# Expert stage of a graph layer: one half of the gated rows turned by VectorE in squares of 32 by 32

## What is computed

```python
xn = _layernorm(x, axis=-1)
x = x + _L0_gnn_ref(xn, src, dst, ...) + _L0_mix_ref(xn[None], ...)[0]
x = x + _L0_ffn_ref(_layernorm(x, axis=-1)[None], L0_ffn_router_w, L0_ffn_w_gate, L0_ffn_w_up, L0_ffn_w_down)[0]
```

```python
logits = flat @ router_w.T
topk_vals, topk_idx = jax.lax.top_k(logits, K)          # K = 2 of E = 8
topk_w = jax.nn.softmax(topk_vals, axis=-1)
dense_w = jnp.zeros((s, E)).at[jnp.arange(s)[:, None], topk_idx].add(topk_w)
g = jnp.einsum('sd,edh->esh', flat, w_gate)             # 512 -> 1024
u = jnp.einsum('sd,edh->esh', flat, w_up)
y = jnp.einsum('esh,ehd->esd', jax.nn.silu(g) * u, w_down)   # 1024 -> 512
out = jnp.einsum('esd,se->sd', y, dense_w)
```

## Time and profile before

| | |
|---|---|
| time before, median of 3 runs | 1580.67 us |
| the profiled execution's own time | 1579.48 us |
| its span, first to last instruction | 1577.8 us |
| TensorE busy | 1401.8 us (89%), 463.05 of the 474 us from 1103 to 1577 |
| VectorE busy | 915.8 us (58%), 147.19 of those 474 us |
| ScalarE busy | 638.9 us (40%), 59.89 of those 474 us |
| GpSimd busy | 757.0 us (48%), 95.69 of those 474 us |
| transposes of the gated rows, L1713 | 168, 26.3 us busy |

### The profile page before, as it was taken

The page is one execution under the profiler, slowest core; times in us unless marked ns, Lnnn a source line. Parts: engine busy times, 40 slices in busy tenths (PEclk is TensorE's granted clock), DMA queues, the critical chain, the costliest instruction groups (busy, mean ns, idle before and its releaser), DMA issues.

```text
span 1577.8 us, 24763 instructions
## 1 busy us (share of the span) xinstructions
PE 1401.8 (89%) x6831; PEld 659.2 (42%) x6832; DVE 915.8 (58%) x2194; ACT 638.9 (40%) x1124; POOL 757.0 (48%) x776
## 2 busy tenths in 40 slices
PE   6566998867769999999999999782999999999997
PEld 4243444334324444444444444462433334433333
DVE  8745665568737777777777777665332233322332
ACT  2354555545426665666656666540111111111111
POOL 3777777777766655666556665102511111111111
PEclk8677999979879999999999999895999999999999
DMA  4875333333268888888888888852123542514512
GB/s 149 321 256 162 112 113 116 115 113 111 102 219 256 248 247 247 251 250 247 247 249 250 250 247 222 262 217 70 21 81 126 186 156 57 180 41 166 187 25 85
DMA packets 130351, 274.52 MB, mean 174 GB/s; under 512 B 21129, under 2 KB 67933, under 8 KB 129346
## 3 DMA queue, kind: packets, MB, share of 16 engines
q0 software_dynamic: 49872, 150.16, 31.8%
q1 hardware_dynamic: 80434, 123.84, 23.5%
HBM read 211.55 MB, written 64.99 MB: 175 GB/s over the span
## 4 chain that ended last, share of the span: by engine, by line
PE 64%; POOL 21%; issue 7%; DVE 3%; DMA 3%; ACT 0%; SPq 0%; DVEq 0%; POOLq 0%; ACTq 0%
POOL edge_list L423 20%; PE psum L1190 19%; PE psum L1706 17%; PE psum L1718 9%; PE psum L1203 7%; PE psum L1198 5%; PE psum L1185 2%; PE psum L1713 1%; POOL slot_list L1638 1%; DMA shared<-node_table,shared 1%; PE psum L1368 1%; DMA z_rows<-z 1%; PE psum L1369 1%; DVE zN L1785 1%; PE psum L1293 1%
## 5 line engine op out<-in xcount | busy, mean ns | idle before, releaser
L1094 POOL DMA_INDIRECT shared<-node_table,shared x343 | 324.3, 945 | 222.3 <-DVE msg L1162 131.2
L423 POOL DMA_INDIRECT edge_list<-rec,place x313 | 316.8, 1012 | 99.6 <-issue 95.1
L1164 DVE TENSOR_TENSOR msg<-shared,psum 128x768 f32<-128x768 f32 x339 | 321.0, 947 | 0.0
L1190 PE MATMUL psum<-wf,hT 128*128 128x512 f32 x678 | 316.0, 609 | 2.0 <-ACT psum L1124 2.0
L1706 PE MATMUL psum<-shared,zT 128*64 128x512 f32 (+1 forms) x960 | 299.7, 598 | 9.6 <-DVE zT L1779 9.4
L1124 ACT COPY psum<-bias 128x512 f32<-128x512 f32 x343 | 202.1, 590 | 227.8 <-DVE msg L1164 209.1
L1162 DVE TENSOR_TENSOR msg<-shared,psum 128x256 f32<-128x256 f32 x339 | 140.7, 415 | 145.5 <-PE psum L1190 142.0
L1190 PEld LDWEIGHTS psum<-wf,hT 128*128 128x128 f32 x678 | 122.8, 191 | 160.0 <-issue 139.7
L1706 PEld LDWEIGHTS psum<-shared,zT 128*64 128x64 f32 (+1 forms) x960 | 112.6, 159 | 179.0 <-issue 169.4
L440 PE MATMUL psum<-wf,fT 128*128 128x512 f32 (+1 forms) x158 | 100.8, 725 | 80.6 <-DVE rec L767 77.2
L1718 PE MATMUL psum<-shared,hidT 128*64 128x512 f32 (+1 forms) x480 | 152.7, 597 | 0.0
(11 more groups left out here) (304 smaller groups left out, 1531.6 us busy)
## 6 DMA issues: line engine op xcount, KB each, us to landing
shared<-edge_list SPq DMA_DIRECT2D x356, 130.0 KB
shared<-in_L_ffn_w_gate SPq DMA_DIRECT2D x8, 2048.0 KB, 8.9
shared<-in_L_ffn_w_up SPq DMA_DIRECT2D x8, 2048.0 KB, 14.2
shared<-in_L_ffn_w_down SPq DMA_DIRECT2D x8, 2048.0 KB, 19.7
shared<-node_table,shared POOLq DMA_INDIRECT x343, 3.8
edge_list<-rec,place POOLq DMA_INDIRECT x313, 2.6
raw<-in_records SPq DMA_DIRECT2D x19, 256.0 KB, 3.5
xrow<-in_x SPq DMA_DIRECT2D x10, 250.0 KB
```

The costliest lines, as they stand in the source:

```text
L423: nc.gpsimd.indirect_dma_start(out=edge_list, out_offset=bass.IndirectOffsetOnAxis(ap=place[:n_, c:c + 1].bitcast(U32), axis=0), in_=rec[: ...
L1094: nc.gpsimd.indirect_dma_start(out=gat[:, k % G, :], out_offset=None, in_=table, in_offset=bass.IndirectOffsetOnAxis(ap=ix, axis=0)).then_ ...
L1164: nc.vector.tensor_tensor(m[:, 1:7, :].rearrange("p (a i) f -> p a i f", a=2), g[:, P:D].rearrange("p (i f) -> p i f", i=3).unsqueeze(1).t ...
L1190: nc.tensor.matmul(WP[k % TS][:], hT[:, (k // TS) % 2, (k % TS) * P:(k % TS + 1) * P], wf2[:], start=False, stop=True, skip_group_check=Tr ...
```

## The change

VectorE turns the first half of the gated rows itself, with sixteen transposes of the kind that it uses for the tokens, straight from `hid` to `hidT`. TensorE's `turn_hidden(0)` and ScalarE's copy of that half are gone; those of the second half stay. The three semaphores count one a block now, and two are new: `hid_first`, on which VectorE waits for its own multiply, and `first_turned`, on which TensorE waits before the first `down` step. The new VectorE work stands between the two multiplies of a block. Elsewhere five semaphores that TensorE raises once each in the first stage become one that counts to five (`once_mm`), with the same waits at the same places; the diff shows one of them.

```diff
@@ first stage: one of five
-                    ins.then_inc(col_mm, 1)
+                    ins.then_inc(once_mm, 1)
...
-                    dve.wait_ge(col_mm, 1)
+                    dve.wait_ge(once_mm, COUNTS)
@@ expert stage, TensorE
                             def turn_hidden(h_):
-                                pe.wait_ge(hid_done, b * 2 + (h_ + 1))
+                                pe.wait_ge(hid_done, b + 1)
...
                             hidden(GATE[1], wgate, 1)
-                            turn_hidden(0)
                             hidden(UP[1], wup, 1)
-                            pe.wait_ge(hid_copied, b * 2 + 1)
+                            pe.wait_ge(first_turned, b + 1)
                             pe.wait_ge(y_bank, b + 1)
                             for m in range(HM // 2 - 1):
                                 down(m)
                             turn_hidden(1)
                             down(HM // 2 - 1)
-                            pe.wait_ge(hid_copied, b * 2 + 2)
+                            pe.wait_ge(hid_copied, b + 1)
@@ expert stage, ScalarE
-                            act.wait_ge(hid_turned, b * 2 + (h_ + 1))
-                            nc.scalar.copy(hidT[:, h_ * DJ:(h_ + 1) * DJ, :], TURNED[h_][:].rearrange("p (q n) -> p q n", q=DJ)).then_inc(hid_copied, 1)
+                        act.wait_ge(hid_turned, b + 1)
+                        nc.scalar.copy(hidT[:, DJ:HM, :], TURNED[1][:].rearrange("p (q n) -> p q n", q=DJ)).then_inc(hid_copied, 1)
@@ expert stage, VectorE
-                            nc.vector.tensor_tensor(hid[:, h_, :], sg[:, h_, :], UP[h_][:], ALU.mult).then_inc(hid_done, 1)
+                            ins = nc.vector.tensor_tensor(hid[:, h_, :], sg[:, h_, :], UP[h_][:], ALU.mult)
+                            if h_ == 0:
+                                ins.then_inc(hid_first, 1)
+                                dve.wait_ge(hid_first, b + 1)
+                                for i in range(BLK // W):
+                                    for q in range(P // W):
+                                        ins = nc.vector.transpose(hidT[q * W:(q + 1) * W, 0:DJ, i * W:(i + 1) * W],
+                                                                  hid[i * W:(i + 1) * W, 0, :].rearrange("t (j p) -> t j p", j=DJ)[:, :, q * W:(q + 1) * W])
+                                ins.then_inc(first_turned, 1)
+                            else:
+                                ins.then_inc(hid_done, 1)
```

More of the change, by code:

```diff
@@ L263, in gps_layer @@
             aoT = vs[:].rearrange("p a g d -> p (a g d)")[:, 0:2 * DJ * CR].rearrange("p (a j n) -> p a j n", a=2, j=DJ)
-            member_s, cast_s, col_mm, counted, tile_mm, based, diag_s, row_mm = (sem(n_) for n_ in (
-                "member_done", "constants_cast", "counts_mm", "tiles_counted", "tile_starts_mm", "bases_done", "diagonals", "rows_mm"))
+            member_s, cast_s, once_mm, counted, based, diag_s = (sem(n_) for n_ in (
+                "member_done", "constants_cast", "single_mm", "tiles_counted", "bases_done", "diagonals"))
+            COUNTS, TILE_STARTS, ROWS, SORTED, TABLES = 1, 2, 3, 4, 5
             pos_mm, pos_read, placed_cols, zero_idx, zeros_made, zeroed = (sem(n_) for n_ in (
@@ L272, in gps_layer @@
                 "squares_done", "inverse_length", "factors_done"))
-            tabs_s, tabs_mm, tabs_done = sem("tables_found"), sem("tables_mm"), sem("tables_done")
-            ranked, sort_mm = sem("buckets_ranked"), sem("sorted_mm")
+            tabs_s, tabs_done = sem("tables_found"), sem("tables_done")
+            ranked = sem("buckets_ranked")
             quad_mm, eq_done, quad_ln, x_read, hot_done = (sem(n_) for n_ in (
@@ L557, in _ @@
                                                start=(b == 0), stop=(b == NB - 1))
-                    ins.then_inc(col_mm, 1)
+                    ins.then_inc(once_mm, 1)
                     pe.wait_ge(counted, 1)
-                    nc.tensor.matmul(bank[MM][:, 320:321], sconst[:, C_TRI2 - NKEEP:C_TRI2 - NKEEP + P], nt[:], start=True, stop=True).then_inc(tile_mm, 1)
+                    nc.tensor.matmul(bank[MM][:, 320:321], sconst[:, C_TRI2 - NKEEP:C_TRI2 - NKEEP + P], nt[:], start=True, stop=True).then_inc(once_mm, 1)
                     pe.wait_ge(diag_s, 1)
                     nc.tensor.matmul(bank[MM][:, 328:328 + 3 * NB], const[:P // 2, C_ONE:C_ONE + P], diag[:].rearrange("p a b -> p (a b)"),
-                                     start=True, stop=True).then_inc(row_mm, 1)
+                                     start=True, stop=True).then_inc(once_mm, 1)
                     turn_edges(0)
@@ L578, in _ @@
                             nc.tensor.matmul(bank[MM][:, 0:3 * NB], const[:P // 2, C_ONE:C_ONE + P], sorted_[:].rearrange("p a b -> p (a b)"),
-                                             start=True, stop=True).then_inc(sort_mm, 1)
+                                             start=True, stop=True).then_inc(once_mm, 1)
                         if u == TABS_AT:
@@ L586, in _ @@
                                     ins = nc.tensor.matmul(TAB[k][0:1, j * P:(j + 1) * P], tb[:, k, j:j + 1], ident, start=True, stop=True)
-                            ins.then_inc(tabs_mm, 1)
+                            ins.then_inc(once_mm, 1)
                         if u in TURN_AT:
@@ L791, in tables @@
                     def tables():
-                        dve.wait_ge(sort_mm, 1)
+                        dve.wait_ge(once_mm, SORTED)
                         link(nc.vector.tensor_copy(nrow[:].rearrange("p a b -> p (a b)"), bank[MM][:, 0:3 * NB]))
@@ L921, in _ @@
                     nc.vector.tensor_copy(nt[:], cnt_i[:]).then_inc(counted, 1)
-                    dve.wait_ge(tile_mm, 1)
+                    dve.wait_ge(once_mm, TILE_STARTS)
                     link(nc.vector.tensor_scalar(off[:], bank[MM][:, 320:321], float(P), float(P), ALU.mult, ALU.add))
@@ L931, in _ @@
                     nc.vector.tensor_copy(base[:], base_i[:]).then_inc(based, 1)
-                    dve.wait_ge(row_mm, 1)
+                    dve.wait_ge(once_mm, ROWS)
                     er_ = bank[MM][:, 328 + 2 * NB:328 + 3 * NB].unsqueeze(1).to_broadcast([P, ZI, NB])
@@ L993, in _ @@
                         if u == TABS_AT:
-                            dve.wait_ge(tabs_mm, 1)
+                            dve.wait_ge(once_mm, TABLES)
                             for j in range(TS):
@@ L1602, in gps_layer @@
             LISTED = 16 * 2 * NC_
-            gated = sem("gated")
+            gated, hid_first, first_turned = sem("gated"), sem("hidden_first"), sem("hidden_first_turned")
             picked_s, ids_mm, ids_found, to_in, stored = (sem(n_) for n_ in (
```

## The result

The changed kernel takes 1576.78 us in the median of 15 runs, the kernel before 1583.22 in the median of 15: a ratio of 0.996, with a 95% interval of 0.9946 to 0.9973. That is about 6.4 us faster where 7.7 were forecast (1573.0). The time itself lies 3.8 us above the forecast and only 0.2 under the upper end of the range (1577); 2.55 us of that came from the kernel before, whose median was 1580.67 in its first three runs and is 1583.22 in fifteen. Of the outcomes that the prediction weighed it is the one within 0.5% (chance 0.51). The span of the profiled execution fell from 1577.8 to 1572.4 us. The expert stage, from its first matmul (1104.23 us after, 1103.82 before) to the end of the span, fell from 474.0 to 468.2 us: **5.8 us**.

What follows compares the result with a forecast made beforehand. TensorE's unbroken row was taken to bound the expert stage: 11.15 us saved in the blocks, less 1.2 (block 1), 0.5 (weights) and 1.8 (clock), gives 7.65, so 1573.0 us against the median 1580.67; range 1569.5 to 1577.

Steps and rivals of the forecast that it cites:

- the one within 0.5%: Whole kernel: the time stays within 0.5% of the kernel before, about 7.9 us, too little to tell from no change; chance 0.51.
- What bounds the stage: Expert stage: TensorE's work is an unbroken chain from the third block on, so whatever leaves its row shortens the span.
- 0.44 a full block, 0.75 a halved one: Savings per block with one expert's weights (full) or two experts' (halved); ten full and nine halved give 11.15 us.
- Rival 4: Expert stage: TensorE's transposes filled a slot that something else fills anyway; 1583.7 us, chance 0.05.
- The cover of VectorE's transposes: Each block: sixteen transposes take 5.05 us, ending 0.38 us before the down load is late and 0.62 before the multiply.
- rival 2: VectorE bounds every block if a transpose takes over 0.355 us start to start; 1594 us at 0.42, chance 0.08.
- Block 1's longer wait: Block 1: VectorE is late, TensorE idles 4.56 us; blocks 0 and 1 together lose 1.2 us rather than give 0.88.
- The clock: Block 1: TensorE's granted clock falls for a while after the longer idle; 1.8 us lost, between 0.95 and 2.75.
- Rival 1: Block 1: the clock stays full, so 9.5 us are saved; 1571.2 us, chance 0.22.
- The weights: Block 16: the next expert's last weight load binds, so its 0.44 is lost; 0.5 us lost, bounds 0.44 and 1.76.
- rival 3: Blocks 3, 6 and 14: their weight loads bind as in block 16, losing 1.3 us more; 1574.3 us, chance 0.07.
- The end of the kernel: Last scatter: released by VectorE's last sum; the copy of sums to the output moves along, so no cost.

Runs made afterwards that it cites:

- run 1: Changed kernel with TensorE's four transposes of the first half put back, their result unread; ratio 1.0008 to the kernel before, expert stage 476.2 us.
- run 6: Changed kernel with one more VectorE transpose, unread, before the first half is given out; ratio 0.9964 to the kernel before, stage 466.9 us.
- run 7: Changed kernel with four more VectorE transposes, unread, before the first half is given out; ratio 1.0029 to the kernel before, stage 477.3 us.
- run 2: Changed kernel with GpSimd's list entries moved forward (3, 6 and 11 for 2, 4 and 14); ratio 0.9926 to the kernel before, stage 461.9 us.
- run 5: Changed kernel with list entries moved forward and a separate semaphore for the down weights; ratio 0.9922 to the kernel before, stage 460.4 us.
- run 8: Changed kernel with only one list entry moved forward (3, 4 and 13); ratio 0.9949 to the kernel before, stage 464.0 us.
- run 10: Repeat of the changed kernel with entries moved forward and a separate down-weight semaphore; ratio 0.9938 to the kernel before, stage 460.4 us.
- run 4: Changed kernel with a separate semaphore for the down weights, waited for only before the first down matmul; ratio 0.9949, stage 466.5 us.
- run 3: Kernel before with GpSimd's list entries moved forward (3, 6 and 11); ratio 0.9977 to the unedited kernel before, stage 471.4 us.

## Why the prediction was right, point by point

- **What bounds the stage.** Right: with TensorE's transposes put back (run 1) the gain is gone, and the rest of the change brings nothing.
- **0.44 a full block, 0.75 a halved one.** Measured 0.44 and 0.73; 10.97 us for 11.15. That a halved block gives more because its transposes stand between matmuls on halves of the array fits the rows, but no run varied it.
- **Rival 4, the change doing nothing for TensorE's row.** Excluded: the blocks are shorter by what was removed, and run 1 takes it back.
- **The cover of VectorE's transposes.** Right: 5.05 us for sixteen, 0.47 between their end and the load for the 0.38 + 0.06 worked out. Run 6 spends most of it without loss, run 7 goes beyond it and loses 9.6 us. That bears out rival 2's mechanism and its point of decision: run 6 amounts to 0.335 us per transpose, run 7 to 0.394, on either side of 0.355. The Trainium skill's figure for VectorE ("VectorE: DVE Perf Modes", section "The three transpose paths") is 311 ns for a 128x128 bf16 block. No run here turns bf16; these fp32 turns took 0.315 us for each 32x128, 5.05 for four 128x128 blocks, and not the 1.24 us estimated from that figure. One sum of the prediction is wrong there: with 1.24 us the half would have been ready at 1142.16, block 1's down matmuls would have started 2.6 us sooner than before, and the saving would have been 11.15 + 2.6 - 0.5 = 13.3 us, not 11.5. The forecast did not rest on it.
- **Block 1's longer wait.** Right in kind and size: the down matmuls start 42.29 us after the stage's start for 40.97, 1.3 later where 1.2 were forecast. The idle was 5.67 us for 4.56, since block 0 ran less of its time at the lower clock (15.34 us to its first down matmul; 16.92 before); its end is not what block 1 waits for, so this only lengthened the idle. In the second trace it was 4.40. The cause of the late multiply, GpSimd's queue, is shown by run 2.
- **The clock.** The mechanism was right: the granted clock fell to 0.54 behind the idle, and with less idle (runs 1, 2, 5, 8, 10) the six records kept their 2.68 us. The Trainium skill ("TensorE: Matmul & The Clock Gate", section "Why this matters for your kernels") says the same of gaps between bursts of matmuls, and the traces agree: 4.40 and 5.67 us of idle lowered it, 2.46 did not. Rival 1, the clock staying full, fell in both traces of the changed kernel. The term was mis-sized in the first trace, 1.8 for 2.65 (5.22 against 2.57), and met in the second, 1.8 (4.37 against 2.57); 0.1 of each is the start behind any wait. That the second fits to a tenth is luck, since 1.8 was no more than the middle of two distant bounds, 0.95 and 2.75.
- **The weights.** Named right, mis-sized: 0.5 for 1.2. I gave block 16 only the 0.44 that it lost and took the landing time of one trace, 20.3 us, for fixed. It was 20.7 in the first trace of the changed kernel, 20.4 in its second and up to 21.3 in the others built on it, so block 17 waits about 1.0, where 0.55 was forecast, and block 4, behind the block 3 that I let off by hundredths, waits 0.27. In the second trace of the changed kernel all four short loads bind and cost 1.8 us: there rival 3, with its chance of 0.07, was what happened, and its price (0.5 + 1.3) was right. A slack of 0.04 us, which is what 0.48 less 0.44 leaves, should have been counted as none. Run 4 gives the whole back.
- **The end of the kernel.** Right: the last scatter was released by VectorE's last sum, after 14.20 us of waiting.

The forecast was 1.3 us of 7.7 too high against the medians and 1.9 against the stage. The clock (0.85), the weights (0.7), the halved blocks (0.2) and block 1's delay (0.1) account for the latter. In the second trace the stage gained 6.2 us: the clock came out as forecast, and the weights took 1.3 more.

What stays open: where between 2.46 and 4.34 us of idle the clock begins to fall in block 1, and what sets how long it stays low; and why the stages ahead of the expert stage were some 150 us longer in the later runs, for the kernel before too. The traces show only that they moved less data a second there (249 GB/s between 600 and 900 us in the kernel before, 220 in the second trace of the changed kernel, with TensorE busy 300 and 276 us). The expert stage does not change with it.

## What to carry to other kernels

Where the matrix engine's row is unbroken, an instruction taken from it is worth its start-to-start time plus the changes of tile shape around it, in every block, and a move to another engine is free only as long as the moved work ends in time for its reader: work out that distance (0.47 us to the reader's load here, some 0.7 with what the load itself can slip), and test it by adding a known piece of work. Look for the one or two iterations at the start of a loop in which the helping engine is late: the moved work stands in full there, and an idle matrix engine pays twice, by the wait and by the clock behind it. A gain also uses up the slack of the transfers beside it, so list those that land within a few tenths of their need, and price them by the spread of their landing times and not by the median.

## What the runs showed of the hardware

- The price of a longer idle of TensorE is not the idle alone: behind 4.34 to 5.97 us of it the next six records took 4.37 to 5.26 us for 2.57. Behind 0.26 to 2.46 us they took 2.68, so 0.1 is the start behind any wait.
- A stall of TensorE costs more than the idle that the trace names: 0.26 us of named idle a block in run 7 was 0.5 us of time, as the first matmul starts 0.4 later (14.16 us for 13.73), and the six records from it on take 0.1 longer (2.68 for 2.57).
- The last of an expert's three weight loads, 2 MB, landed 19.4 to 21.3 us after its issue in the loop over experts. The load issued in block 16 alone took from 19.8 us (run 3) to 21.3 (run 5), and 20.7 and 20.4 in the two traces of one kernel.
- VectorE's transposes of what it has just written took 299 to 309 ns, the same as those of gathered tokens (292 to 308), and the wait on its own multiply cost 0.03 us.
